# A gated and reordered opening in a two-block adapter kernel

## The reference

```
# block 0: a linear layer and a gated mixture of 8 low-rank adapters (rank 16)
base   = x @ W.T                                   # W: 512 x 512
logits = x @ Wr.T + 5.0 * one_hot(language_id)     # 8 experts, one id for each batch
gates  = softmax over the two largest logits, scattered back to 8
h      = x @ A[e].T for all experts                # 8 x 16 = 128 numbers
x1     = x + base + 2.0 * sum_e gates[e] * (h[e] @ B[e].T)
# block 1: one of 64 adapters for each batch (rank 16)
out    = x1 + (x1 @ B1[adapter_id].T) @ A1[adapter_id].T
```

## Time and profile before

| | us |
|---|---|
| median of three runs | 99.25 |
| lowest, highest | 99.24, 99.54 |
| the profiled execution | 99.71 |
| its span, first to last instruction | 97.4 |
| TensorE busy | 92.1 |
| VectorE busy | 62.2 |
| ScalarE busy | 43.7 |
| POOL busy | 37.4 |

### The profile page before, as it was taken

One profiled execution on the slowest core, in us unless ns is written; L12 is line 12 of the kernel. 1 busy time (PEld: TensorE's weight loads), 2 busy tenths in 40 slices (PEclk: granted clock), 3 DMA queues, 4 the chain that ended last, 5 costly groups with the idle time before them and its releaser, 6 DMA issues.

```text
span 97.4 us, 2162 instructions
## 1 busy us (share of the span) xinstructions
PE 92.1 (95%) x733; PEld 77.5 (80%) x733; DVE 62.2 (64%) x215; ACT 43.7 (45%) x88; POOL 37.4 (38%) x44
## 2 busy tenths in 40 slices
PE   4997899999999999999999999999999999999960
PEld 1596788889978788888978898889978897898950
DVE  4163999822297939891089749890199569881980
ACT  2552559240699991089207990099019700000300
POOL 5000778998920049995000069990000370000000
PEclk9999999999999999999999999999999999999999
DMA  1999947438983594235522922227000003241066
GB/s 20 353 279 340 429 156 224 97 73 271 382 202 83 124 367 93 51 71 159 153 60 47 344 98 108 108 50 274 5 0 0 3 7 127 88 172 43 7 211 220
DMA packets 14987, 14.36 MB, mean 147 GB/s; under 512 B 10112, under 2 KB 11392, under 8 KB 14592
## 3 DMA queue, kind: packets, MB, share of 16 engines
q1 hardware_dynamic: 14048, 11.85, 37.9%
q0 software_dynamic: 640, 2.10, 6.9%
q10 hardware_dynamic: 288, 0.28, 1.1%
HBM read 10.02 MB, written 4.19 MB: 146 GB/s over the span
## 4 chain that ended last, share of the span: by engine, by line
PE 84%; DMA 6%; DVE 4%; SPq 1%; ACT 1%; issue 0%; DVEq 0%
PE main L635 16%; PE main L641 15%; PE main L647 15%; PE aw_ps L677 11%; DMA xs<-x_t 6%; PE side L729 6%; PE main L662 4%; PE main L661 4%; PE main L663 4%; PE aw_ps L753 3%; DVE xs L530 2%; PE side L709 2%; PE main L753 1%; PE side L753 1%; SPq L212 1%; DVE x_lo L441 1%
## 5 line engine op out<-in xcount | busy, mean ns | idle before, releaser
L318 POOL TENSOR_TENSOR x_lo<-xs,x_hi 128x512 fp32r<-128x512 f32 x12 | 16.1, 1379 | 19.9 <-ACT x_hi L338 19.9
L635 PE MATMUL main<-x_hi,w_hi 128*128 128x512 f32 (+1 forms) x64 | 17.7, 398 | 0.5 <-DVE w_hi L565 0.5
L641 PE MATMUL main<-x_hi,w_lo 128*128 128x512 f32 (+1 forms) x64 | 16.9, 385 | 0.0
L647 PE MATMUL main<-x_lo,w_hi 128*128 128x512 f32 (+1 forms) x64 | 16.8, 384 | 0.0
L677 PE MATMUL aw_ps<-aws,xs 128*128 128x136 f32 x112 | 14.6, 284 | 0.0
L677 PEld LDWEIGHTS aw_ps<-aws,xs 128*128 128x128 f32 x112 | 14.2, 195 | 0.2
L370 ACT ACTIVATE a_ops<-a_hi 64x512 fp32r<-64x512 f32 x12 | 7.6, 630 | 14.5 <-POOL a_rest L292 14.3
L641 PEld LDWEIGHTS main<-x_hi,w_lo 128*128 128x128 f32 x64 | 11.8, 188 | 2.6
L647 PEld LDWEIGHTS main<-x_lo,w_hi 128*128 128x128 f32 x64 | 11.8, 188 | 2.4
L635 PEld LDWEIGHTS main<-x_hi,w_hi 128*128 128x128 f32 x64 | 11.3, 188 | 2.9 <-DVE w_hi L565 0.7
L489 DVE TENSOR_TENSOR xs<-main,xs 128x512 f32<-128x512 f32 x15 | 9.9, 683 | 2.1 <-PE main L663 2.1
(11 more groups left out here) (107 smaller groups left out, 136.2 us busy)
## 6 DMA issues: line engine op xcount, KB each, us to landing
out_t<-xs SPq DMA_DIRECT2D x16, 256.0 KB, 2.2
xs<-x_t SPq DMA_DIRECT2D x3, 1024.0 KB, 5.3
b1s<-b_t SPq DMA_DIRECT2D x64, 32.0 KB, 2.1
xs<-x_t SPq DMA_DIRECT2D x4, 256.0 KB, 4.1
ws<-w_t SPq DMA_DIRECT2D x4, 256.0 KB, 6.3
b0s<-b_t SPq DMA_DIRECT2D x1, 256.0 KB, 6.5
aws<-aw_t ACTq DMA_DIRECT2D x1, 204.0 KB, 3.9
rows<-a_t,row_at POOLq DMA_INDIRECT x8, 3.6
```

The lines of the kernel that those rows point to most:

```text
L318: nc.gpsimd.tensor_tensor(x_lo[:, t % 2, c], xs[:, t, c], x_hi[:, t % 2, c].bitcast(F32), ALU.subtract).then_inc(x_lo_ready, 1)
L635: nc.tensor.matmul(out_ap, w_hi[:, c, k], x_hi[:, s, k, n], start=(k == 0), stop=False)
L641: nc.tensor.matmul(out_ap, w_lo[:, c, k], x_hi[:, s, k, n], start=False, stop=False)
L647: last = nc.tensor.matmul(out_ap, w_hi[:, c, k], x_lo[:, s, k, n], start=False, stop=False)
```

## The change

The two tables of ids become one tensor with one load. SP now waits for the second piece of x's tile 0 ahead of column 1 of w and the ids, for the third ahead of column 2 and `b0s`, and for the fourth ahead of column 3 and tile 1 of x. VectorE makes the remainders of pieces 2 and 3 (counted from 0) after its work on column 0 of w, and `w_rest(3)` ahead of `gate_h(0)`. POOL waits for `b0_lo_ready` ahead of the first remainder of tile 1.

```diff
+        ids = sb("ids", [P, IDS + NB * TILES], I32)
+        adapter_ids, language_ids = ids[:, 0:IDS], ids[:, IDS:]
...
             sp.dma_start(ws[:, 0], w[:, 0]).then_inc(w_loaded[0], 16)
-            sp.dma_start(language_ids[:], language_id.rearrange("p (t j) -> p t j", t=NB)).then_inc(language_loaded, 16)
-            sp.dma_start(adapter_ids[:], adapter).then_inc(adapter_loaded, 16)
+
+            sp.wait_ge(x0_loaded[1], 16)
             sp.dma_start(ws[:, 1], w[:, 1]).then_inc(w_loaded[1], 16)
+            sp.dma_start(ids[:], id_table).then_inc(ids_loaded, 16)
+            sp.wait_ge(x0_loaded[2], 16)
             sp.dma_start(ws[:, 2], w[:, 2]).then_inc(w_loaded[2], 16)
             sp.dma_start(b0s[:], b0).then_inc(b0_loaded, 16)
+            sp.wait_ge(x0_loaded[3], 16)
             sp.dma_start(ws[:, 3], w[:, 3]).then_inc(w_loaded[3], 16)
             sp.dma_start(xs[:, 1], x[:, 1]).then_inc(x_loaded[1], 16)
...
                     for c in range(K):
                         pool.wait_ge(x_hi_ready, t * K + c + 1)
+                        if t == 1 and c == 0:
+
+                            pool.wait_ge(b0_lo_ready, 1)
...
-            for c in range(K):
+            def x0_rest(c):
                 dve.wait_ge(x_hi_ready, c + 1)
                 split_lo(x_lo[:, 0, c], xs[:, 0, c], x_hi[:, 0, c], x0_lo_ready)
+
+            x0_rest(0)
+            x0_rest(1)
             dve.wait_ge(w_loaded[0], 16)
             nc.vector.tensor_copy(w_hi[:, 0], ws[:, 0]).then_inc(w0_hi_ready, 1)
             dve.wait_ge(w0_hi_ready, 1)
             split_lo(w_lo[:, 0], ws[:, 0], w_hi[:, 0], w0_lo_ready)
-
-            dve.wait_ge(language_loaded, 16)
+            x0_rest(2)
+            x0_rest(3)
+
+            dve.wait_ge(ids_loaded, 16)
...
             w_rest(1)
             top_two(0)
             pick()
             w_rest(2)
+            w_rest(3)
             gate_h(0)
-            w_rest(3)
             dve.wait_ge(b0_hi_ready, 1)
             split_lo(b0_lo[:], b0s[:], b0_hi[:], b0_lo_ready)
             gt_rest(0)
```

More of the change, by code:

```diff
@@ L51, with two_block_kernel @@
 WARM = 6
-def two_block_kernel(nc, x, adapter, language_id, w, aw, b0, a1, b1, out, *, tokens_per_batch,
+def two_block_kernel(nc, x, id_table, w, aw, b0, a1, b1, out, *, tokens_per_batch,
                      experts, rank, adapters):
@@ L131, in two_block_kernel @@
         IDS = NG + NG * BPG
-        adapter_ids = sb("adapter_ids", [P, IDS], I32)
+        ids = sb("ids", [P, IDS + NB * TILES], I32)
+        adapter_ids, language_ids = ids[:, 0:IDS], ids[:, IDS:]
         wrap = sb("wrap", [P, IDS], I32)
@@ L137, in two_block_kernel @@
         row_at = sb("row_at", [P, NG], I32)
-        language_ids = sb("language_ids", [P, NB, TILES], I32)
         is_language = sb("is_language", [P, NB, TILES, experts])
@@ L143, in two_block_kernel @@
         side = [psum(f"side{i}") for i in range(2)]
-        adapter_loaded, language_loaded = sem("adapter_loaded"), sem("language_loaded")
+        ids_loaded = sem("ids_loaded")
         x0_loaded = [sem(f"x0_loaded{c}") for c in range(K)]
@@ L292, in split_a1 @@
                 nc.gpsimd.tensor_tensor(lo, rows[:, s], hi.bitcast(F32), ALU.subtract).then_inc(a1_lo_ready, 1)
-            pool.wait_ge(adapter_loaded, 16)
-            nc.gpsimd.tensor_scalar(wrap[:], adapter_ids[:], 0.0, float(adapters), ALU.is_lt,
+            pool.wait_ge(ids_loaded, 16)
+            nc.gpsimd.tensor_scalar(wrap[:], adapter_ids, 0.0, float(adapters), ALU.is_lt,
                                     ALU.mult).then_inc(index_step, 1)
             pool.wait_ge(index_step, 1)
-            nc.gpsimd.tensor_tensor(wrapped[:], wrap[:], adapter_ids[:], ALU.add).then_inc(index_step, 1)
+            nc.gpsimd.tensor_tensor(wrapped[:], wrap[:], adapter_ids, ALU.add).then_inc(index_step, 1)
             pool.wait_ge(index_step, 2)
@@ L567, in _ @@
             split_lo(w_lo[:, 0], ws[:, 0], w_hi[:, 0], w0_lo_ready)
-            dve.wait_ge(language_loaded, 16)
+            x0_rest(2)
+            x0_rest(3)
+            dve.wait_ge(ids_loaded, 16)
             then_wait(nc.vector.tensor_tensor(
                 is_language[:].rearrange("p t j e -> p (t j) e"),
-                language_ids[:].rearrange("p t j -> p (t j)").unsqueeze(2).broadcast_to([P, NB * TILES, experts]),
+                language_ids.unsqueeze(2).broadcast_to([P, NB * TILES, experts]),
                 expert_no[:].unsqueeze(1).broadcast_to([P, NB * TILES, experts]), ALU.is_equal))
@@ L839 @@
         "x_t": x.reshape(NB, TB, K, P).transpose(3, 0, 2, 1),
-        "adapter": np.concatenate([np.repeat(adapter.reshape(-1, P // R).T, R, axis=0),
-                                   np.broadcast_to(adapter.reshape(1, B), (P, B))], axis=1),
-        "language_id": np.repeat(language.reshape(-1, P // T).T, T, axis=0),
+        "id_table": np.concatenate([np.repeat(adapter.reshape(-1, P // R).T, R, axis=0),
+                                    np.broadcast_to(adapter.reshape(1, B), (P, B)),
+                                    np.repeat(language.reshape(-1, P // T).T, T, axis=0)], axis=1),
         "w_t": w.reshape(K, P, K, P).transpose(3, 0, 2, 1),
```

## The result

The changed kernel takes 100.16 us (median of 10 runs, 99.69 to 100.52) against 99.25 for the kernel before (10 runs, 98.73 to 99.66): ratio 1.0092, 95% interval 1.0070 to 1.0113. The profiled execution took 100.01 us, with a span of 98.2.

The account below looks back on a forecast made before the run. TensorE, 95% busy, was taken as bound by its first projection's start, then by POOL's chain at tile 1's transposes. The opening's win counted nothing; profiled 99.71 plus D 1.3 gave 101.0 us, range 99.9 to 102.4.

Parts of the forecast that it names:

- POOL's chain: Tile 1's x_lo, a_rest, ScalarE's packing and exp, VectorE's gate, TensorE's transposes: no slack, so POOL's lateness reaches the transposes.
- the opening's win: First projection at 9.1 instead of 10.0, up to 0.9 us; worth nothing if D is above zero.
- The sum along the chain: b0_lo written at C + 9.1, POOL's x_lo of tile 1 ended at C + 14.25, chain late by C - 7.2.
- C: Landing of column 0 of w (ws0), which starts VectorE's cast: taken as 8.5, bounds 7.35 to 9.5, forecast 7.8 to 9.1.
- D: Lateness of POOL's chain at tile 1, C - 7.2: 1.3 us, bounds 0.15 to 2.3.
- rival 2: Load queue runs clean, C near 7.4, D 0.2, opening's win unused: 99.9 us; chance 0.13.
- The profiled time as the base: Whole kernel: the sum starts from the profiled 99.71 us, 0.46 above the median 99.25.
- Rival 1: Opening loads: holding them back does nothing, column 0 still lands at 9.5, D 2.3: 102.0 us; chance 0.25.
- Rival 3: First projection starts at 9.1 and the transposes don't hold TensorE: 98.8 us; chance 0.08.
- Rival 4: A 2.2 us stall at the transposes drops TensorE's clock to half rate, up to 2.3 us more: 103.3; chance 0.08.
- The stall of about 2 us: Sign of being right: TensorE held by gated for about 2 us ahead of the second tile's transposes.
- a_rest over 1 us later: Sign of being right: POOL's a_rest starts over 1 us later than 23.84.

Follow-up runs that it names:

- the six of the table: Profiles of the kernel before (first profile and e0), the changed kernel, e2, e3, and the changed kernel without POOL's wait (99.84 us).
- e10: Changed kernel with VectorE's gap subtraction of tile 1 moved behind tile 0's three add_x1 (second link cut): 100.17 us, ratio 1.0094.
- e14: The kernel of e9 run again in another job: 98.73 us, ratio 0.9947.
- e9: Changed kernel with both links cut (gap subtraction behind the add_x1, exp between the two groups of packing copies): 98.27 us, ratio 0.9916.
- e5: Changed kernel with ScalarE's exp_gap(1) ahead of tile 0's eight packing copies (first link cut): 99.30 us, ratio 0.9999.
- e3: Changed kernel without SP's three waits: 100.75 us, ratio 1.0132.
- e2: Kernel before with only POOL's wait for b0_lo_ready added: 99.72 us, ratio 1.0055.
- e11: Kernel before with both links cut as in e9, nothing of the change: 98.51 us, ratio 0.9920.
- e4: Changed kernel without SP's three waits and without POOL's wait: 105.04 us (99.7 to 105.6).
- e0: Kernel before again, only a blank line added, for a second profile: 99.11 us, ratio 0.999.

## Why the prediction was right, by its steps

- *POOL's chain sets the time, and the opening's win is worth nothing*: shown. The transposes of tile 1 start 10.73 to 10.77 after x_lo's end in all seven profiles that have the exp behind the packing and no long stall before it (the six of the table and e10). Cutting both links gave back 1.4 to 1.9 us (e14, e9), cutting one gave 0 (e10) or 0.9 (e5).
- *The sum along the chain*: b_lo ended at 16.68, where C + 9.1 with the cast at 7.73 gives 16.8; x_lo ended at 21.87, predicted C + 14.25 = 21.98; D = C - 7.2 gives 0.5 and the trace shows 0.42 at the transposes, where 1.3 was forecast.
- *C = 8.5*: this term was mis-sized. It measured 7.7, between the forecast's band (7.8 to 9.1) and rival 2 (7.35). With it the same sum gives 99.71 + 0.5 = 100.2, and 100.16 was measured. The step of 1.0 from 9.5 to 8.5 was about the right size for the gates; the start was off. Without gates C is 8.1 to 9.5 in seven profiles, in the middle 8.5, and with them 7.3 to 7.9, in the middle 7.7: the kernel before was profiled in the latest of its openings. That the time still came to lie in the range is owed to a range wide enough for rival 2.
- *The profiled time as the base*: it served for the time, because the sum counts from x_lo's end in that same execution (the same sum gives 101.3 for e3 and 99.9 for e2, whose profiled executions took 101.10 and 99.69), and it hid part of the loss. Counted from the medians the change cost 0.9, while the two first profiles differ by 0.4 at the transposes and 0.3 in time: the profiled execution of before was 0.46 above its median. Where a usual execution of before is shorter, the second profile (99.58, the same span) doesn't show either; an earlier x_lo, as in e11 (14.34), would do it, and stays a guess.
- *Rival 1* (ring order in the Trainium skill's "DMA: Bandwidth & Descriptors", Queues, rings and completion order) is refuted as a forecast: with the loads behind it held back column 0 of w landed 4.7 to 5.2 us after its issue instead of 5.4 to 6.8, worth 0.4 to 0.6 us of time. By what way, no run here shows. The page's rule itself isn't refuted: it is on the order in which an engine takes descriptors, and the same sentence says that a later one may finish its write before an earlier one, so the rule alone didn't fix C at 9.5.
- *Rival 2* (C near 7.4, 99.9 us) came as near to the measurement as the forecast's band did: C 7.7, and D 0.4 where it had 0.2.
- *Rival 3*, the opening's win, did not come: the first projection did start at 9.1 and it was worth nothing. With both links gone the times are near the 98.8 computed for it (98.27 in e9, 98.73 in e14), but so is the kernel before with the same cuts (98.51), so this isn't shown to be a win of the change's opening.
- *Rival 4* is refuted for the stall that it was priced for, 2.2 us: after the stalls of 0.53 and of 2.26 us (e10) four matmuls still take 1.17, at a granted clock of 1.00. After 4.43 us (e4) they ran at 0.50. The Trainium skill's "TensorE: Matmul & The Clock Gate" (The HAM clock gate) names idling as the cause; the rows agree for the long stall alone.
- *The stall of about 2 us*, given as a sign of being right, was 0.53: C was smaller than forecast, and 0.6 of TensorE's lead had gone before, at the gap. So was "a_rest over 1 us later": it was 0.40.
- *Missed*: the second link. The prediction priced POOL and VectorE getting in each other's way by large operations (1.77 against 0.69) and not by a tiny one that stands until POOL's instruction ends. It didn't change the sum, because the first link hid it: with the second alone cut the time stayed at 100.17 (e10).

## What to carry to other kernels

Ask where the run behind an opening is tight before pricing the opening: a faster start is worth nothing when a later join waits for an engine whose chain began elsewhere. Look at small instructions in an in-order program that stand behind long ones of another kind (the exp behind eight copies) or run beside another engine's long ones (the gap beside a_rest), and move those first. A hold that keeps two engines apart should be checked for what queues behind it: here it cost 0.6 us in the kernel before, and guarded against a loss of 3 to 6 that only one of the kernels without it showed (e4). And one profile is one execution: the 0.9 that the opening seemed to have to give was mostly a late landing in the execution profiled, as a second profile of the same kernel showed.

## What the runs showed of the hardware that was not expected

Two small operations of VectorE, with operands in SBUF, did not share with POOL's two-input subtractions but stood until these ended. The gap subtraction took 0.32 (e0), 0.70 (e2), 0.97 (the changed kernel), 1.29 (e5) and 2.11 us (e3), against 0.15 to 0.17 alone, each time ending 0.02 to 0.04 after a_rest. The addition of denom, with one input, took 5.33 (e4; 0.16 to 0.30 elsewhere) and ended 0.03 after four x_lo in a row. Not all small ones stand: the four MAX8 just ahead of the gap in the changed kernel took 0.38 beside a_rest (25.43 to 25.81) and 0.37 in the kernel before, when a_rest was over. Large subtractions beside POOL took 1.26 to 1.79 instead of 0.69. The Trainium skill's "GPSIMD Engine Reference" (Specifications) says the SBUF interfaces are shared with VectorE, with contention for instructions with two SBUF inputs or in a two-port mode; for the gap the rows agree, and they show a size: the whole rest of POOL's run of subtractions, over several instructions, here up to 5 us. Whether denom ran in a two-port mode, no run here shows.

The load of a column of w landed 4.7 to 5.2 us after its issue where the loads behind it were held back, and 5.4 to 6.8 where they were not (seven profiles each).
